# Causal attention: the second head's normalisation moves from GpSimd to ScalarE

## The reference, cut to what matters

```python
xn = layernorm(x) * ln_gamma + ln_beta
q, k, v = split(xn @ w_qkv.T)              # 16 heads of 64
sim = (q * 64 ** -0.5) @ k.T               # per head, 1024 x 1024
sim = where(causal, -max_float, sim)
attn = softmax(sim, axis=-1)
x = x + (attn @ v) @ w_out.T + b_out
```

## Time and profile before

| | us |
|---|---|
| median of 3 runs | 3648.4 (3647.82 to 3649.07) |
| the profiled execution, its own time | 3644.16 |
| its span, first to last instruction | 3642.4 |
| PE busy | 3169.9 (87%) |
| DVE busy | 2107.0 (58%) |
| ACT busy | 2088.0 (57%) |
| POOL busy | 1727.0 (47%) |

### The profile page before, as it was taken

How to read it: one execution, slowest core, us unless ns; L and a number is a source line. 1 busy time by engine, 2 the same in 40 slices (tenths; PEclk the granted TensorE clock), 3 DMA queues, 4 the chain that set the end, 5 groups by cost and what they waited for, 6 DMA issues and landing times. The chain is left out here.

```text
span 3642.4 us, 72895 instructions
## 1 busy us (share of the span) xinstructions
PE 3169.9 (87%) x26438; PEld 1944.9 (53%) x26564; DVE 2107.0 (58%) x4204; ACT 2088.0 (57%) x3388; POOL 1727.0 (47%) x1348
## 2 busy tenths in 40 slices
PE   6599999858889988749999999999996688999885
PEld 4222222535566656526666666666664455666663
DVE  4200000458887777555555555555555688777773
ACT  2499999425555555435555555555553455555552
POOL 1100000058888888513333333333332788888882
PEclk9799999979999999979999999999998899999998
DMA  1122221021111111000000000000000211111111
GB/s 33 21 38 39 36 39 30 7 81 34 33 34 34 35 35 34 22 10 9 6 9 6 9 6 9 6 9 6 7 7 29 63 36 33 35 36 36 35 32 32
DMA packets 124405, 95.70 MB, mean 26 GB/s; under 512 B 80448, under 2 KB 100544, under 8 KB 123968
## 3 DMA queue, kind: packets, MB, share of 16 engines
q1 hardware_dynamic: 122784, 89.41, 11.2%
q10 hardware_dynamic: 1440, 3.80, 0.3%
HBM read 22.90 MB, written 2.10 MB: 7 GB/s over the span
## 5 line engine op out<-in xcount | busy, mean ns | idle before, releaser
L1737 POOL TENSOR_SCALAR e<-e,inv 128x768 f32<-128x768 f32 (+7 forms) x512 | 375.1, 745 | 763.6 <-DVE inv L1629 763.6
L1700 ACT ACTIVATE e<-e,nmax 128x768 f32<-128x768 f32 (+7 forms) x512 | 395.4, 772 | 429.6 <-DVE e L1624 427.1
L1624 DVE TENSOR_SCALAR_CACHE_REDUCE e<-slot 128x768 f32<-128x768 f32 (+7 forms) x512 | 376.5, 754 | 242.6 <-PE slot L1513 242.6
L530 ACT ACTIVATE e<-slot 128x1024 f32<-128x1024 f32 x512 | 472.5, 1087 | 38.0 <-PE slot L466 38.0
L880 POOL TENSOR_TENSOR inv_norm<-floored,minus_half 128x16 f32<-128x16 f32 x128 | 374.1, 2923 | 10.7
L1617 DVE COPY eT<-slot 128x512 f32<-128x512 f32 (+3 forms) x384 | 239.0, 622 | 235.4 <-PE slot L1524 235.3
L1117 ACT ACTIVATE probT<-slot 128x1024 f32<-128x1024 f32 x128 | 131.1, 1024 | 376.4 <-PE slot L973 376.4
L1524 PE MATMUL slot<-ident,e 128*128 128x128 f32 x2304 | 332.9, 280 | 8.4 <-DVE eT L1617 3.5
L852 POOL TENSOR_TENSOR prob<-prob,inv_total 128x1024 f32<-128x1024 f32 x128 | 242.7, 1896 | 200.4 <-DVE inv_total L1209 200.4
L1507 PE MATMUL slot<-key,q 64*128 64x512 f32 (+3 forms) x1536 | 318.1, 518 | 19.2 <-ACT v L1687 12.8
L873 POOL TENSOR_TENSOR rot<-cosine,sine 128x1024 f32<-128x1024 f32 x128 | 301.9, 2359 | 53.3 <-DVE sine L1191 53.2
(11 more groups left out here) (158 smaller groups left out, 6443.7 us busy)
## 6 DMA issues: line engine op xcount, KB each, us to landing
v_mix<-v SPq DMA_DIRECT2D x256, 128.0 KB, 2.3
w_qkv<-in_causal_w_dram SPq DMA_DIRECT2D x32, 192.0 KB
query<-q_hi SPq DMA_DIRECT2D x128, 32.0 KB
keys<-q_hi SPq DMA_DIRECT2D x128, 32.0 KB
query<-q_lo SPq DMA_DIRECT2D x128, 32.0 KB
keys<-q_lo SPq DMA_DIRECT2D x128, 32.0 KB
hs<-H SPq DMA_DIRECT2D x32, 128.0 KB
h1s<-H SPq DMA_DIRECT2D x32, 128.0 KB
```

The lines of the kernel that those rows point to most:

```text
L530: act.activation(e[n % E_RING][:], c.slots[n % RING][:].rearrange(flat), ACT.Exp, scale=2 * SCALE).then_inc(e_ready, 1)
L1624: dve.tensor_scalar(e[n % RING][h][:, 0:cols], c.slots[h][:].rearrange(flat)[:, 0:cols], -1.0, None, ALU.mult, ALU.min, accum_out=nmax[:, ...
L1700: act.activation(part, part, ACT.Exp, bias=nmax[:, n, h:h + 1], scale=-1.0, accum_out=total[:, n, h:h + 1]).then_inc(e_ready, 1)
L1737: pool.tensor_scalar(part, part, inv[:, n, h:h + 1], 1.0, ALU.mult, ALU.mult).then_inc(scaled, 1)
```

## The change

The second head's product moves to ScalarE's queue. There it is an `activation` with the function Copy and the reciprocal as a scale for each row. It stands in the step behind its own: in step n, right behind the exponential of head 0, ScalarE scales step n - 1 of head 1. In steps 1, 3 and 5 that is ahead of both projection copies. GpSimd keeps head 0. The one semaphore becomes two, so that TensorE waits for each head by itself. After the last step ScalarE scales that step's head 1 before the last copies.

```diff
-        scaled = sem("scaled")
+        scaled = [sem("head0_scaled_pool"), sem("head1_scaled_act")]
...
                 def transpose(u, n, h, first):
-                    pe.wait_ge(scaled, 2 * TICKS * u + 2 * n + h + 1)
+                    pe.wait_ge(scaled[h], TICKS * u + n + 1)
...
+                def scale(u, n):
+                    part = e[n % RING][1][:, 0:(tile_of(n) + 1) * P]
+                    act.wait_ge(inv_ready, TICKS * u + n + 1)
+                    act.activation(part, part, ACT.Copy, scale=inv[:, n, 1:2]).then_inc(scaled[1], 1)
...
                         exp(u, n, 0)
+                        if n > 0 or not first:
+                            us, ks, ns = earlier(u, k, n - 1)
+                            scale(us, ns)
                         if not last and n in PROJECT:
                             project_out(u + 1, PROJECT[n][0], 1 - k)
...
                 u = UNITS - 1
+                scale(u, TICKS - 1)
...
-                def scale(u, n, h):
-                    part = e[n % RING][h][:, 0:(tile_of(n) + 1) * P]
-                    if h == 0:
-                        pool.wait_ge(inv_ready, TICKS * u + n + 1)
-                        pool.sem_inc(inv_seen, 1)
-                    pool.tensor_scalar(part, part, inv[:, n, h:h + 1], 1.0, ALU.mult, ALU.mult).then_inc(scaled, 1)
+                def scale(u, n):
+                    part = e[n % RING][0][:, 0:(tile_of(n) + 1) * P]
+                    pool.wait_ge(inv_ready, TICKS * u + n + 1)
+                    pool.sem_inc(inv_seen, 1)
+                    pool.tensor_scalar(part, part, inv[:, n, 0:1], 1.0, ALU.mult, ALU.mult).then_inc(scaled[0], 1)
...
                     for n in range(TICKS):
-                        scale(u, n, 0)
-                        scale(u, n, 1)
+                        scale(u, n)
```

## The result

The changed kernel took 3730.5 us (median of 4 runs, 3729.28 to 3732.11) against 3648.1 us (4 runs); the ratio is 1.0226, 95% interval 1.0208 to 1.0244. It is slower, by 82 us; forecast were 83. The profiled execution took 3729.28 us, its span is 3727.5 us.

What follows compares the result with a forecast made beforehand. TensorE was taken to bound the loop; 30 units at 2.71 us (81.3) plus 0.8 and 0.5 for the end units gave 82.6, say 83 us, so 3731 us. Range 3700 to 3785, or 3717 to 3743 if only the price is in doubt.

Steps and rivals of the forecast that it cites:

- What bounds the loop: Attention loop: TensorE, busy 98%, sets the pace, so every us it is made to wait is a us of the kernel.
- The price of one product: ScalarE's queue: a product holds it for its duration less 0.10, 1.05 us at 1024 columns to 0.61 at 512.
- The stalls of a unit: TensorE's waits behind the products of steps 1, 3 and 5: 1.02 + 0.86 + 0.83 = 2.71 us on 36.50.
- lower price of 72 us: Lower bound of the total cost: four products 0.09 us cheaper each, 2.35 us a unit.
- The second stall of step 0 to 1: TensorE waits about 0.5 us for step 0's head 1 product; covered by the 1.02, costing 0.5 without that cover.
- The first and the last unit: Loop ends: 0.8 us in the first unit, from step 5 alone, and 0.5 in the last, from step 1's wait.
- No cost in steps 2, 4, 6 and 7: Products there push head 1's exponential by 0.2 to 0.8 us but cost nothing; tightest is step 7, 0.5 us of cover.
- What is removed is worth nothing: GpSimd's 256 second products, waited for 3.4 us in all: counted 0, bounds 0 and -3.4.
- The clock: Rival: TensorE's larger idle pockets lower its clock once in each unit, 53 us more, 3784 us; chance 0.10.
- The uncovered wait: Rival: step 1's 0.5 us wait adds to the 1.02, or thin covers give way; 15 more, 3746 us; chance 0.12.
- ScalarE hides it: Rival: second projection copies in steps 1, 3, 5 have 1.0 us or more to spare, stalls vanish, 3643 us; chance 0.06.
- The turning point: Slack in the odd steps at which hiding the product is decided: about 0.9 us, against 0.21, 0.08 and none read.

Runs made afterwards that it cites:

- the run with the immediate: Changed kernel with the product's scale an immediate 1.0 in place of the reciprocal for each row, head 1 left not normalised: 3716.0 us, ratio 1.0189 to before.
- The idle time kernel: Changed kernel with head 1's product behind the second projection copy in odd steps, ahead of head 0's exponential in even ones: 3647.0 us, ratio 1.0006 to before.
- the narrow run: Changed kernel with only head 1's narrow products (128 to 512 columns, even steps) on ScalarE, GpSimd keeping the wide ones: 3660.5 us, ratio 1.0042 to before.
- the kernel with the exchange and halves: Kernel before with step 5's second v copy ahead of head 1's exponential and head 0's 1024-column GpSimd product in two halves: 3631.7 us, ratio 0.9964.

## Why the prediction was right

**What bounds the loop** (every wait of TensorE is paid): held. The same work in idle time costs nothing, and 0.09 us in the chain is paid in full.

**The price of one product**: held. 1.05, 0.94, 0.83 and 0.61 us of the queue were forecast; the measured durations less 0.10 are 1.03, 0.93, 0.82 and 0.61. The operand at 0.09 was inferred, and the run with the immediate shows 0.092. The Trainium skill, "ScalarE: Activation LUTs", section "What ACT_TABLE_LOAD costs", gives about 93 ns, and these rows agree.

**The stalls of a unit**: 1.02, 0.86 and 0.83 were forecast. Steps 0 to 2 lost 0.61 + 0.43 = 1.04, step 3 lost 0.82, step 5 0.82. Sum 2.71 forecast, 39.17 - 36.50 = 2.67 measured, and the loop 81.2 us for 82.6. (One slip of the working: its lower price of 72 us gives 3720 us as the lower end, not 3717.)

**The second stall of step 0 to 1**: mis-sized and partly misread. It was put at 0.5 us, from the end of the product plus the signal. What ends it is the copy of bank 1 behind the product, which I had counted only as delaying the exponential: 2132.13 + 0.61 + 0.26 + 0.13 = 2133.13, where 2132.5 was the start before, 0.6 us, and 0.61 is measured. That it is covered when both are there held (changed kernel: 1.04, not 1.6). That it would cost its full size without the cover did not: 0.38 of 0.62, because the kernel before already waits about 0.2 us at the next transposes for head 0's product. The step that missed it is the reading of the rows: the scores of step 2 began "behind the transposes", and I took these for TensorE's own work.

**The first and the last unit**: 0.8 and 0.5 us were forecast, 0.30 and 0.65 measured, and that they are near is luck. The granted clock differs between the two traces there. Busy time by stretch, columns as in the earlier trace rows; first and last unit before, then first unit, steady part and last unit after:

```profile
1617.00:1653.00 36.00, 29.55 (x179) 17.29 (x179) 16.89 (x47) 19.24 (x45) 11.31 (x16) 0.91 0.05 14
2748.00:2796.00 48.00, 42.06 (x341) 28.52 (x341) 26.18 (x64) 19.43 (x49) 13.08 (x18) 0.96 0.01 3
```

```profile
1617.00:1655.00 38.00, 27.52 (x187) 16.68 (x187) 17.92 (x49) 23.61 (x54) 7.29 (x9) 1.00 0.05 13
1655.00:2829.00 1174.00, 1077.17 (x8160) 709.26 (x8156) 655.36 (x1678) 762.32 (x1740) 207.21 (x269) 1.00 0.02 7
2829.00:2878.00 49.00, 42.50 (x343) 28.85 (x341) 26.55 (x64) 26.00 (x61) 6.65 (x9) 0.97 0.01 3
```

The first unit took 36.03 us before and 36.33 in the changed kernel, but 33.26 without the second product, a trace with the clock at 1.00 there, like the changed kernel's. At the same clock the change costs 3.07 us in this unit: 0.75, 0.82 and 0.83 in the intervals 1 to 2, 3 to 4 and 5 to 6 (3.83, 3.53 and 3.98 without the product), and 0.28 and 0.39 in 2 to 3 and 4 to 5. "Steps 1 and 3 cost nothing" was wrong, and the lower clock of the trace before hid 2.8 us of it. The loop of the kernel before has three short stretches at the lower clock, that of the changed kernel one, in its last unit. The idle time kernel has one too, and its loop takes 1175.5 us; against that the changed kernel loses 84.6.

**No cost in steps 2, 4, 6 and 7**: held; in the steady part those intervals didn't move by more than 0.02 us.

**What is removed is worth nothing**: held. Without the second product at all the ratio is 0.9997.

**The rivals.** *The clock*: its granted share stayed at 1.00 from 1655 to 2829 us, with three idle times of 0.6 to 1.2 us and one of 0.5 in each unit. The Trainium skill, "TensorE: Matmul & The Clock Gate", section "A second HAM failure mode: psum-queue depth-cycling", reports a kernel whose clock went back and forth between its levels because of small idle times between groups of matmuls; pockets of this length and spacing didn't bring that about here. The rival was rightly held unlikely, but not for the reason given, that the new pockets are shorter than 1.58 us: the last section has a fall behind 1.42. *The uncovered wait*: not in the changed kernel; alone, it is what the narrow run shows. *ScalarE hides it*: wrong for this place in the queue, right for another, which the run in idle time shows. The turning point was read correctly: what counts is the slack of the odd steps' projection copies, not ScalarE's idle share.

## What to carry to other kernels

An engine that is busy 57% of the time can still be the wrong place for more work: read the slack of the instructions behind the insertion point in its own queue, down to the one for which the bounding engine waits. The same eight instructions cost 82 us with the wide ones ahead of the projection copies, 14 with these behind the copies, and nothing that could be measured when in addition the narrow ones stood ahead of an exponential that waits for its input anyway. A list of waits isn't complete: compare the interval between two fixed points of the bounding engine's queue across kernels, since a wait called "issue" can be one for a neighbour. And compare the same units: a difference of single traces at the ends of a loop can be the clock's, here up to 2.8 us.

## What the runs showed of the hardware

An idle time ahead of TensorE's weight load is put down to "issue" in the rows although the instruction waited for GpSimd: about 0.2 us in each unit, found only when the product was made shorter (0.18 of it ahead of the transposes).

The clock: in the last unit before the change, 1.85 us of TensorE's idle time was followed by a fall; in the same place the changed kernel idled 1.40 us, and the four microseconds behind show 1.00. The length of the idle time alone doesn't decide it. In the idle time kernel 1.84 us was followed by no fall, and in the kernel with the exchange and halves 1.42 us was. The rows, with the granted clock behind each (columns as in the earlier trace rows), are first of the one and then of the other:

```profile
2756.24 1.09 PE L1524 MATMUL slot<-ident,e 128*128 128x128 f32 x8 [1.84 <-POOL e L1747]
2757.00:2761.00 4.00, 4.00 (x34) 2.55 (x33) 2.52 (x6) 1.59 (x4) 0.37 (x1) 1.00 0.02 4
```

```profile
2745.43 1.54 PE L1527 MATMUL slot<-ident,e 128*128 128x128 f32 x8 [1.42 <-POOL e L1747]
2746.00:2750.00 4.00, 3.90 (x13) 1.76 (x14) 0.76 (x2) 0.60 (x1) 1.83 (x4) 0.57 0.01 4
```

What does decide it isn't shown here. In the steady part of the loop the granted clock is 1.00 in the traces of all the kernels.
